# Attention rows of a graph network: gathers that skip padding by an index bound, small loads begun earlier, more row buffers

## The reference

```python
enh = node_features + 0.1 * query_emb[None, :]
Q = (enh @ Wq + bq).reshape(N, H, D); K, V likewise
rel = rel_w[edge_relations]
mod_k = K[src] + 0.2 * rel[:, None, :]
scores = jnp.einsum('ehd,ehd->eh', Q[dst], mod_k) / D ** 0.5
seg_max = jax.ops.segment_max(scores, dst, num_segments=N)
ex = jnp.exp(scores - seg_max[dst])
denom = jax.ops.segment_sum(ex, dst, num_segments=N)
agg = jax.ops.segment_sum((ex / denom[dst])[:, :, None] * V[src], dst, num_segments=N)
```

## Time and profile before

| | |
|---|---|
| median of 3 runs | 6590.93 us (6588.28 to 6594.62) |
| the profiled execution, its own time | 6596.38 us |
| its span | 6594.6 us |
| busy share of the span: TensorE, its weight loads, VectorE, ScalarE, GpSimd | 69%, 48%, 53%, 27%, 50% |
| mean granted TensorE clock | 0.823 of full speed |
| moved by DMA | 926.04 MB, 140 GB/s over the span |

### The profile page before, as it was taken

The page is one execution under the profiler, slowest core; times in us unless marked ns, Lnnn a source line. Parts: engine busy times, 40 slices in busy tenths (PEclk is TensorE's granted clock), DMA queues, the critical chain, the costliest instruction groups (busy, mean ns, idle before and its releaser), DMA issues. The chain is left out here.

```text
span 6594.6 us, 77889 instructions
## 1 busy us (share of the span) xinstructions
PE 4536.3 (69%) x20233; PEld 3165.4 (48%) x20234; DVE 3516.4 (53%) x7039; ACT 1798.7 (27%) x5528; POOL 3267.1 (50%) x2372
## 2 busy tenths in 40 slices
PE   3787797796865555655555537532992699998978
PEld 3455575574652434433334423321561377776446
DVE  8574755745426666666666656661113444443245
ACT  0232332323311444444444430010220122221122
POOL 0011786885876555555555547666554444442000
PEclk9888899898888767777777768756996899999989
DMA  7998313213124656566656844323992455554000
GB/s 232 310 359 280 69 2 73 27 2 93 2 16 116 174 169 177 173 173 171 172 172 172 169 96 117 108 52 120 308 316 76 141 199 195 199 198 145 0 24 20
DMA packets 775991, 926.04 MB, mean 140 GB/s; under 512 B 383219, under 2 KB 636182, under 8 KB 771496
## 3 DMA queue, kind: packets, MB, share of 16 engines
q1 hardware_dynamic: 348392, 633.65, 28.2%
q0 software_dynamic: 417328, 281.90, 20.5%
q10 hardware_dynamic: 10128, 8.79, 0.4%
HBM read 682.29 MB, written 240.09 MB: 140 GB/s over the span
## 5 line engine op out<-in xcount | busy, mean ns | idle before, releaser
L741 POOL DMA_INDIRECT pairs<-REC,FARC x800 | 1663.7, 2080 | 1096.7 <-DMA pairs<-REC,FARC 479.7
L1016 PE MATMUL a_pa<-a_VW,identf 128*128 128x260 f32 x1920 | 741.4, 541 | 109.5 <-issue 102.3
L916 POOL DMA_INDIRECT a_KV<-kv_tab,KEYS x600 | 580.2, 967 | 399.6 <-ACT a_VW L978 187.8
L1004 PE MATMUL a_pq<-QS,a_ohT 128*128 x720 | 167.8, 358 | 656.0 <-DVE a_otT L932 397.1
L1016 PEld LDWEIGHTS a_pa<-a_VW,identf 128*128 128x128 f32 x1920 | 490.0, 268 | 240.5 <-issue 124.8
L916 POOL DMA_INDIRECT XN<-kv_tab,KEYS x360 | 345.7, 960 | 257.4 <-ACT a_VW L978 156.5
L1004 PEld LDWEIGHTS a_pq<-QS,a_ohT 128*128 128x128 bf16 x720 | 79.3, 110 | 780.3 <-issue 758.2
L978 ACT ACTIVATE a_VW<-a_KV,a_VW 128x64 f32<-128x64 f32 x1800 | 447.9, 339 | 4.9
L2284 DVE TENSOR_TENSOR AIN<-AIN,w_pin 128x512 f32<-128x512 f32 (+1 forms) x325 | 216.7, 667 | 425.9 <-PE w_pin L2323 420.0
L1701 PE MATMUL m_bank<-m_QK,m_VX 128*128 128x320 f32 x1280 | 358.2, 439 | 3.6 <-ACT m_QK L1591 3.6
L1692 PE MATMUL m_bank<-m_VX,m_QK 128*128 128x256 f32 x1600 | 356.9, 384 | 2.5 <-ACT m_QK L1597 2.5
(11 more groups left out here) (565 smaller groups left out, 9365.0 us busy)
## 6 DMA issues: line engine op xcount, KB each, us to landing
pairs<-ZERO SPq DMA_DIRECT2D x32, 5000.0 KB, 40.4
e_W<-in_L_ffn_w SPq DMA_DIRECT2D x192, 512.0 KB
REC<-pairs SPq DMA_DIRECT2D x100, 800.0 KB, 7.0
RES<-pairs SPq DMA_DIRECT2D x13, 3200.0 KB, 10.2
HB<-pairs SPq DMA_DIRECT2D x12, 3200.0 KB, 10.3
m_crow<-cell_tab SPq DMA_DIRECT2D x75, 488.3 KB
row_tab<-a_arow SPq DMA_DIRECT2D x240, 130.0 KB
n_AR<-row_tab SPq DMA_DIRECT2D x30, 1040.0 KB, 5.2
```

What stands on the lines that cost most here:

```text
L741: pool.indirect_dma_start(self.pairs[half], bass.IndirectOffsetOnAxis(self.FARC[:, i:i + 1].bitcast(I32), 0), self.REC[:, i, 0:4].bitcast( ...
L916: pool.indirect_dma_start(KV[t % UB][:, j, :], None, self.kv_tab, bass.IndirectOffsetOnAxis(self.SIDX[:, t * ROW + j:t * ROW + j + 1], 0)) ...
L1004: pe.matmul(pq[b][:, 0:D], ohT[:, h, g, :], QS[:, at(k), j, :], start=j == 0, stop=j == 2)
L1016: last = pe.matmul(sums[b], self.identf[:, :], VW[:, b, e, :, :], start=e == 0, stop=e == ROW - 1)
```

## The change

1. `order_rows` copies the indices without the minimum, so filling slots keep 4095. Each gather gets `bounds_check=N - 1, oob_is_err=False`: a row whose index is above 3124 is not fetched, and its place in the buffer stays as it was. So that this place holds numbers, GpSimd clears each of the five own buffers before its first gather and waits for the clearing.
2. The node and relation numbers are loaded into four buffers (`AHEAD = 4`) in place of two. SyncE's wait before the load is now for `s_oh`, the one-hots that last read the buffer, in place of `s_q`. The store of finished sums stands ten blocks behind in SyncE's order in place of six, and its loop peels two rounds.
3. `AU` is 8 in place of 4: eight row buffers and semaphores for the store.

```diff
-                    dve.tensor_scalar(self.SIDX[:, :], SIDX[:, :, :].rearrange("r p b -> r (p b)"), float(N - 1), None, ALU.min)
+                    dve.tensor_copy(self.SIDX[:, :], SIDX[:, :, :].rearrange("r p b -> r (p b)"))
...
-        AU, OWN = 4, 5
-        s_bc = [n(f"a_bc{i}") for i in range(2)]
+        AU, OWN, HB2, AHEAD = 8, 5, 2, 4
+        s_bc, s_clr = [n(f"a_bc{i}") for i in range(AHEAD)], n("a_clr")
...
-            dlb, tyb = sb("dlb", [P, 2, HB2, P], BF16), sb("tyb", [NREL, 2, HB2, ROW * P], BF16)
+            dlb, tyb = sb("dlb", [P, AHEAD, HB2, P], BF16), sb("tyb", [NREL, AHEAD, HB2, ROW * P], BF16)
...
-                            h = r // HB2 % 2
-                            need(sp, s_q, t - HB2)
+                            h = r // HB2
+                            need(sp, s_oh, i * AHEAD + (h - AHEAD + 1))
...
-                        on, t, r = tile(i, u, 6, UB, RB)
+                        on, t, r = tile(i, u, 10, UB, RB)
...
-                    steps(sp, RB, UB, 6, step)
+                    steps(sp, RB, UB, 10, step, 2)
...
+                        if t < OWN:
+                            pool.memset(KV[t], 0.0).then_inc(s_clr, 1)
+                            pool.wait_ge(s_clr, t + 1)
                         for j in range(ROW):
-                            pool.indirect_dma_start(KV[t % UB][:, j, :], None, self.kv_tab, bass.IndirectOffsetOnAxis(self.SIDX[:, t * ROW + j:t * ROW + j + 1], 0)).then_inc(s_got[t % UB], 16)
+                            pool.indirect_dma_start(KV[t % UB][:, j, :], None, self.kv_tab, bass.IndirectOffsetOnAxis(self.SIDX[:, t * ROW + j:t * ROW + j + 1], 0),
+                                                    bounds_check=N - 1, oob_is_err=False).then_inc(s_got[t % UB], 16)
...
-                    def onehots(t, h, seen):
-                        dve.wait_ge(s_bc[h], seen)
+                    def onehots(t, g, seen):
+                        h = g % 2
+                        dve.wait_ge(s_bc[g], seen)
                         need(dve, s_q, t - HB2)
-                        dve.tensor_scalar(ohT[:, h, :, :], dlb[:, h, :, :], self.pcol[:, :], None, ALU.is_equal)
-                        dve.tensor_scalar(otT[:, h, :, :], tyb[:, h, :, :], self.pcol[0:NREL, :], None, ALU.is_equal).then_inc(s_oh, 1)
+                        dve.tensor_scalar(ohT[:, h, :, :], dlb[:, g, :, :], self.pcol[:, :], None, ALU.is_equal)
+                        dve.tensor_scalar(otT[:, h, :, :], tyb[:, g, :, :], self.pcol[0:NREL, :], None, ALU.is_equal).then_inc(s_oh, 1)
...
-                            onehots(t, r // HB2 % 2, i * (8 * UB) + 32 * (r // (2 * HB2) + 1))
+                            onehots(t, r // HB2, i * 32 + 32)
```

More of the change, by code:

```diff
@@ L865, in att_rows @@
             "set", "rel", "oh", "q", "k", "sc", "d", "ex", "va", "vw", "a", "ev"))
-        AU, OWN = 4, 5
-        s_bc = [n(f"a_bc{i}") for i in range(2)]
+        AU, OWN, HB2, AHEAD = 8, 5, 2, 4
+        s_bc, s_clr = [n(f"a_bc{i}") for i in range(AHEAD)], n("a_clr")
         s_got, s_out = self.soft_sems("a_got", UB), self.soft_sems("a_out", AU)
-        HV, HB2 = 1, 2
+        HV = 1
         with ExitStack() as c:
```

## The result

The changed kernel takes 6546.69 us (median of 4 runs, 6541.02 to 6549.6), the kernel before 6592.77 in the same comparison (4 runs, 6588.28 to 6606.7). The ratio is 0.9926, 95% interval 0.9908 to 0.9943: faster by 0.7%. The forecast was 6546. The total was right; the place in which it expected the gain was not.

What follows compares the result with a forecast made beforehand. It took the attention rows to be bound by gather issue alternating with the rest of the pipeline, TensorE's counts arriving late. Terms -45 + 0 + 0 from 6590.9 gave 6546 us; own range 6524 to 6578 (0.42), wide range 6440 to 6740.

Steps and rivals of the forecast that it cites:

- The bound of the stage: Attention rows: back-to-back gathers hold TensorE's results until a pause of about 2.4 us; 7.41 us a block against 5.40 unhindered.
- rival 3: Much faster: thinner runs break the hold in real blocks too, 6441; or waits are loads or stores, 6126; chance 0.09.
- The gathers of padding alone, -45,: Last 24 blocks of the stage: gathers that move nothing hold nobody, so blocks run at 5.40 us, 45 us less.
- Rival 2: No change: skipped gathers still take 0.95 us and hold TensorE, or the bound's cost cancels the gain; 6591 to 6601; chance 0.17.
- The real gathers, 0: 868 gathers of blocks with edges: no wait ends on data, the bound's cost unknown between 82 us less and 955 more; taken 0.
- each 0.01 us is 8.7 us: Gather issue is on the path, so 0.01 us on each of 868 real gathers changes the time by 8.7 us.
- signs of being wrong: L916 mean above 1.0 us; three-block runs and 6 us waits from block 217; pace below 7.2 in 2400 to 3600 us.
- signs of being right: First 868 gathers stay 0.95 us, packets vanish after block 217, 5.4 us blocks from 210, stage some 45 us shorter.
- The memsets: Five clearing memsets at the stage's start, 1.8 us each by slope: between +17 and -22 us, taken as 0.
- Loads 0: Small loads six blocks ahead in four buffers: L931 idles only 8.5 us in 162 blocks, none waiting for the load; 0.
- row buffers 0: Eight row buffers: ScalarE's waits at L984 end with VectorE's, 0.09 us apart, so worth 0.
- The Trainium skill's price of data-dependent branching: About 12 cycles an element on GpSimd: if the bound branches, 0.16 us a gather, 139 us in all, sum about 6685.

Runs made afterwards that it cites:

- The fourth comparison: On another chip, the changed kernel without this stage's scatters (issued in the last stage) against the kernel before: 6179.64 against 6157.74 us, ratio 1.0033.
- my memsets: One or three one-column memsets after each gather in the kernel before: ratios 1.0038 and 1.004; one in the changed kernel: 0.9929, each against the kernel before.
- the last experiment: The changed kernel without the scatters in this stage, issued in the last stage instead: 6179.64 us, ratio 1.0033 against the kernel before.

## Why the prediction came out right, and where it was wrong

**The bound of the stage** was read rightly: VectorE's own pace is 5.4 us, 2.0 us a block are lost to TensorE's counts arriving late, and the small loads wait for the same. The fourth comparison bears it out: where the stall is absent the kernel before takes 6158, though no trace of it was taken there; the prediction had written 6126 for these waits gone (under rival 3, for another cause).

**The gathers of padding alone, -45,** failed. The step was that the hold goes with the engine's work of moving rows. Measured: 5 us in these blocks, and with nearly every row skipped the stalls stay (7.06 us a block). Rival 2 had this mechanism, "the hold follows the issue, not the data"; it was right on the data, whether the issue or the packets hold is open, and it was wrong that nothing else would change.

**The real gathers, 0, with "each 0.01 us is 8.7 us",** failed twice. The gather grew by 0.035 and 0.059 us (967 to 1002, 960 to 1019), which by that rule is 868 x 0.045 = 39 us more; and the 240 blocks became 43 us faster. The sum treated the stage as a row of runs and stalls of fixed length and left out that their number, and where the scatter falls among them, can change: 2.8 stalls in eight blocks became 2.5, and the scatter left its place behind a stall. The bound alone gives the gain, with nothing skipped (0.9925), and 46 stalls in the same window. So the total agreed with the forecast by luck: a gain that I had not foreseen (42.5 us in blocks 9 to 217) has the size of one that did not come. Two of the prediction's signs of being wrong came: the tail keeps its runs and 6 us waits, and a gather's mean is above 1.0. One of its signs of being right did not: the packets don't vanish after block 217, their number being the same in all.

**The memsets** took 1.8 us each, as the slope said, and did release TensorE's counts; a later wait of 15.56 us gave the gain back: by the ninth block 3 us more counted from the first block, 7 us more counted from GpSimd's start, inside the bounds of -22 and +17, near the 0 taken.

**Loads 0, row buffers 0**: measured 1.0003 and 0.9983. The second is a small gain that the prediction didn't have, about 11 us, and none of it is seen on top of the bound's: the whole change stands at 0.9926, the gathers' part alone at 0.9918, each inside the other's interval.

**The Trainium skill's price of data-dependent branching** ("GPSIMD Engine Reference", 3.1), by which the sum would have been 6685 if the bound were such a branch, is not borne out for the bound: the bounded gather costs 0.035 to 0.059 us where the estimate had 0.16, and the kernel is faster.

**What stays open.** How the bound shifts the rhythm: the greater distance (1.25 to 1.30 us) or another property of the instruction; my memsets did not bring the distance to 1.30, and the last comparison had no stalls. Open is also whether the scatter's place among the runs is a cause of the gain or goes along with it. Whether the changed kernel is faster at all where the stall doesn't exist was not run: what ran there had the scatters moved behind the stage, and was 0.33% slower. Why TensorE's counts come late while GpSimd issues is open too. The kernel before without scatters (0.990) is a single run, so it is not shown to beat the change.

## What to carry to other kernels

When two parts of a pipeline take turns, don't add up their times for a forecast: find the rhythm (how many blocks lie between two stalls, and what stands right behind one), since an edit that makes a piece longer can still shift the rhythm to its good. Work that an engine does right after a long wait may be on the path in full, and the same work elsewhere in its order free; look at what ended the idle time before it, and move the work to test it. And a right total proves no mechanism: the parts run singly, and the bound with nothing to skip, showed that the gain came from none of the reasons given for it.

## What the runs showed of the hardware

- With a bound an indirect gather of 128 rows of 2 KB takes 1.00 to 1.02 us on GpSimd in place of 0.96, whether it skips nothing (1002 and 1014 ns), a tenth, or nearly all rows (1001 and 1018). The queue has the same number of packets in all three (417328), and its bytes fall with the rows skipped: 281.90, 235.13, 30.84 MB.
- While GpSimd issues gathers one after another, TensorE's semaphore counts can reach VectorE, ScalarE and SyncE 5 us late and more (2448.38 us for matmuls recorded at 2443.09). It doesn't depend on the bytes that the gathers move: the stalls stay at 30.84 MB. It was there in three comparisons and absent in the fourth; the kernel before took 6157.74 there and 6584.63 to 6644.44 in the others.
- A one-column memset between two gathers takes 0.12 us and leaves their distance at 1.25 us; it runs in the 0.30 us gap. A memset of 128 x 2048 float32 took 1.81 us (median; 2.09 us mean into XN) and 0.79 us from its end to the next gather that waits for it.
- In this stage the granted TensorE clock was 0.71 in the changed kernel, in which TensorE pauses with the stalls, and 0.81 in the last experiment, in which it does the same work in 1313 in place of 1741 us.
